# A two-layer convolutional attention kernel: the piece of the next projections moved ahead of the first turned tile

## The reference, cut to what matters

```python
xs = x.reshape(b, c, seq).transpose(0, 2, 1)
qkv = xs @ Wqkv + bqkv
q, k, v = jnp.split(qkv, 3, axis=-1)
...
scores = jnp.einsum('bhqd,bhkd->bhqk', q, k) / jnp.sqrt(jnp.asarray(HEAD_SIZE, x.dtype))
attn = jax.nn.softmax(scores, axis=-1)
out = jnp.einsum('bhqk,bhkd->bhqd', attn, v)
...
x = x + _L0_conv_ref(_gn(x), L0_conv_Wqkv, L0_conv_bqkv, L0_conv_Wout, L0_conv_bout)
x = x + _L1_conv_ref(_gn(x), ...)
```

## Time and profile before

| | |
|---|---|
| median of 3 runs | 3008.57 us (3002.29 to 3011.41) |
| the profiled execution, its own time | 3005.0 us |
| its span, from the first to the last instruction | 3003.2 us |
| mean granted clock of TensorE | 0.971 |
| busy share of PE, DVE, ACT, POOL | 92%, 73%, 55%, 7% |
| share of the chain that ended last: PE, DVE, ACT, DMA | 73%, 12%, 5%, 4% |

### The profile page before, as it was taken

How to read it: one execution, slowest core, us unless ns; L and a number is a source line. 1 busy time by engine, 2 the same in 40 slices (tenths; PEclk the granted TensorE clock), 3 DMA queues, 4 the chain that set the end, 5 groups by cost and what they waited for, 6 DMA issues and landing times.

```text
span 3003.2 us, 60746 instructions
## 1 busy us (share of the span) xinstructions
PE 2771.4 (92%) x25208; PEld 1948.6 (65%) x25208; DVE 2201.0 (73%) x2934; ACT 1665.8 (55%) x2429; POOL 197.3 (7%) x157
## 2 busy tenths in 40 slices
PE   6999799999999999999999999999999999998858
PEld 5666576756667577665776667765677756765434
DVE  5676577687875877868877778768787588775856
ACT  2653466375653755636665556636566375554625
POOL 0000001000200002000020000200020000200300
PEclk9999899999999999999999999999999999998968
DMA  5233012421233112340224311232123311105040
GB/s 202 66 74 107 36 43 76 135 81 45 59 95 130 48 54 60 89 174 8 65 59 134 113 43 39 80 130 86 45 52 101 131 48 54 38 12 175 13 110 29
DMA packets 149602, 235.85 MB, mean 79 GB/s; under 512 B 78609, under 2 KB 97556, under 8 KB 145460
## 3 DMA queue, kind: packets, MB, share of 16 engines
q1 hardware_dynamic: 148468, 219.39, 23.7%
q10 hardware_dynamic: 864, 12.58, 1.2%
HBM read 177.08 MB, written 54.84 MB: 77 GB/s over the span
## 4 chain that ended last, share of the span: by engine, by line
PE 73%; DVE 12%; ACT 5%; DMA 4%; issue 4%; another core or an unknown queue 1%; SPq 0%; DVEq 0%; POOL 0%; ACTq 0%
PE banks L708 12%; PE banks L648 10%; PE banks L677 9%; PE banks L695 8%; PE banks L638 6%; PE banks L894 5%; PE banks L750 5%; PE banks L904 4%; PE banks L896 4%; PE banks L895 4%; DMA recips_dram<-recips 3%; DVE neg_max L1432 3%; DVE exps_turned L1443 2%; ACT exps L1111 2%; PE banks L867 2%
## 5 line engine op out<-in xcount | busy, mean ns | idle before, releaser
L1432 DVE TENSOR_REDUCE neg_max<-banks 128x1 f32<-128x1024 f32 x512 | 601.8, 1217 | 88.8 <-PE banks L677 86.0
L1111 ACT ACTIVATE exps<-banks,neg_max 128x1024 f32<-128x1024 f32 x512 | 566.8, 1113 | 47.4 <-DVE neg_max L1432 46.3
L1123 ACT ACTIVATE exps_turned<-banks 128x1024 f32<-128x1024 f32 x256 | 262.3, 1025 | 553.2 <-PE banks L695 544.9
L1443 DVE COPY exps_turned<-banks 128x1024 f32<-128x1024 f32 x256 | 313.2, 1223 | 262.3 <-PE banks L695 247.5
L677 PE MATMUL banks<-qk_halves 64*128 64x512 f32 x3072 | 432.9, 412 | 60.7 <-ACT exps L1111 39.6
L708 PE MATMUL banks<-exps_turned,values 128*64 128x256 f32 x4096 | 481.1, 384 | 0.8 <-issue 0.8
L695 PEld LDWEIGHTS banks<-ident,exps 64*128 64x128 f32 x8192 | 311.5, 139 | 199.1 <-issue 171.3
L695 PE MATMUL banks<-ident,exps 64*128 64x64 f32 x8192 | 366.6, 228 | 31.4 <-DVE exps_turned L1443 27.3
L708 PEld LDWEIGHTS banks<-exps_turned,values 128*64 128x64 f32 x4096 | 280.3, 137 | 138.8 <-issue 5.1
L677 PEld LDWEIGHTS banks<-qk_halves 64*128 64x128 f32 x3072 | 292.4, 189 | 109.9 <-issue 75.8
L1613 DVE SCALAR_TENSOR_TENSOR qk_halves<-banks,qk_halves 128x1024 fp32r<-128x1024 f32 x256 | 302.0, 1219 | 67.2 <-ACT qk_halves L1160 66.9
(11 more groups left out here) (187 smaller groups left out, 3388.9 us busy)
## 6 DMA issues: line engine op xcount, KB each, us to landing
wqk_ring<-wqk_split SPq DMA_DIRECT2D x62, 512.0 KB
wo_halves<-wo_split_dram SPq DMA_DIRECT2D x8, 2048.0 KB, 7.8
exps_turned<-in_x SPq DMA_DIRECT2D x32, 512.0 KB, 5.6
x_dram<-exps SPq DMA_DIRECT2D x32, 512.0 KB, 2.6
exps_turned<-x_dram SPq DMA_DIRECT2D x32, 512.0 KB, 6.0
out<-exps_turned SPq DMA_DIRECT2D x32, 512.0 KB, 2.6
recips_b<-recips_dram SPq DMA_DIRECT2D x240, 64.0 KB, 3.4
x_image<-in_x SPq DMA_DIRECT2D x14, 1024.0 KB, 7.0
```

The lines of the kernel that those rows point to most:

```text
L1111: freed(act.activation(PB[:, 2 * h + n % 2], slot(("s", m, i)), ACT.Exp, bias=NM[:, m:m + 1], accum_out=SS[:, m:m + 1]), ("s", m, i))
L1432: dve.tensor_reduce(NM[:, m:m + 1], slot(("s", m, i)), AX.X, ALU.max, negate=True).then_inc(mx, 1)
L1443: dve.tensor_copy(PT[:, n // 2 % 2, 1, :, P * j:P * j + P].rearrange("p k (r q) -> p k r q", r=2), TB.rearrange("p r (k q) -> p k r q", k= ...
```

## The change

In the loop over steps on PE, the two lines that issue the piece of the next projections move up: they stood behind the first turned tile and the value products, and now stand between the scores and the first turned tile. Nothing else is edited.

```diff
                     elif i + 1 < B:
                         values(0, i + 1)
+                    if piece_of(n + 1):
+                        piece(n + 1, i)
                     turn(n, 0, i)
                     if n == 0:
                         piece(0, i)
...
                     if (2 <= n < 22 and n % 2 == 0) or (n > 22 and n % 2):
                         value_product(n // 2 - 1, 1, i)
-                    if piece_of(n + 1):
-                        piece(n + 1, i)
                     if i and n == 25:
```

## The result

The changed kernel takes 3300.64 us, the median of four runs (3297.57 to 3303.23); the kernel before took 3005.43 us on the same chip in four runs (2989.46 to 3011.41). The ratio is 1.0988, with an interval of 1.0964 to 1.1013: 10% slower. The prediction said 3338 us. The profiled execution took 3303.23 us, with a span of 3301.4 us and a mean granted clock of 0.942, against 0.971 before.

A forecast was written before the change was run, and what follows sets the result against it. In steps with a piece, PE's order and ACT's copy-exp-exp chain were taken to bound the kernel, ending together. 259.6 - 14.2 + 4 = 249.4; 3005.0 + 249.4 + 84 for clock falls = 3338 us, range 3250 to 3380.

The forecast's parts named there:

- The step itself: In 88 steps with a piece, the first turned tile and ACT's work come 2.95 us later: 8.67 for 5.72, 259.6 us added.
- The two waits: PE waits 1.22 us for ACT's copy and 1.47 us for the exps in each changed step, at no further cost.
- What is given back: In 20 steps the piece covers the first turned tile's wait for DVE's copy: 14.2 us off, bounds nothing and 27.3.
- The piece's wait for its bank: In step 1 of each image the piece waits about 0.5 us for DVE's low part: 4 us added.
- The falls of the clock: TensorE's clock falls to half in 55 of 88 changed steps, at 1.52 us each: 84 us, bounds 0 and 134.
- the eight cases behind it: Earlier places in the trace with like waits on PE: five of eight fell, 0.63, the share taken for the 88 steps.
- bound by PE's own 6.37 us: The step after one with a piece is set by PE's order at 6.37 us, so DVE's 0.37 us gain stays hidden.
- the prediction's own signs of being wrong: ACT's exps starting before the copy's end, the piece running beside the transposes, or even steps taking under 6.37 us.
- The rival of a give-back: Row maxima bound the following step; their earlier start returns 0.37 us in each of 88, falls hide: 3221 us, chance 0.07.
- The rival without falls: The two waits, split by a turned tile, bring no fall of TensorE's clock: 3254 us, chance 0.18.

## Why the prediction was right

The sign and the mechanism were right. The time lies inside the range, 37 us below the value given. Point by point:

- *The step itself.* 8.67 us was predicted, 8.63 measured. ACT's order is the cause: with the exps ahead of the copy the scores' wait is gone, and with half of the piece moved the delay is half. The first turned tile came 4.52 us behind the scores (894.84 to 899.36), 0.04 us earlier than 1.61 + 2.95.
- *The two waits.* Predicted 1.22 and 1.47 us, measured 1.21 and 1.48; in total 110.0 against 3 + 107 for the copy, 165.9 against 39.6 + 129 for the exps.
- *What is given back.* 14.2 us of the waits for DVE's copy was predicted, 16.2 came (27.3 to 11.1). The piece's wait for its bank was put at 4 us, and is 4.9.
- *The falls of the clock.* 55 of 88 at 1.52 us was predicted. In 54 of 88 the scores behind a piece took over 1.75 us. Of the 73 following steps with a whole value product and no work of the second layer on PE, 27 took 6.21 us or less and 46 took 7.59 or more, and these 46 are the ones with slow scores. The typical ones differ by 7.72 - 6.20 = 1.52 us. That the falls are the cause was shown by filling the waits: 78, 84 and 76 us come back (81, 87 and 79 when each kernel is taken against the kernel before on its own chip), against 54 x 1.52 = 82. That the share came out so near, 55 and 54, is luck: of the eight cases behind it only one had the two waits of a changed step, and the experiments show that one wait of this length behind a piece brings no fall.
- *The term that was mis-sized.* The prediction took the following step as "bound by PE's own 6.37 us" and so gave back nothing there. At full clock it takes 6.20 us after the change: 0.17 x 88 = 15 us less. This is one of the prediction's own signs of being wrong, an even step below 6.37 us. With both waits filled, where there are no falls, the steps behind a piece add up to 550.2 us, 19.4 less than before; 2.6 of these are waits for DVE's copy that went. The two chains of the earlier trace rows do not end exactly together, as the prediction read them. The scores at 820.01 were recorded as starting before the turned tile ended at 820.20; this part of their time is PE's excess over ACT's chain, and the first 0.17 us of the delay cost nothing. With half a piece left out the excess goes too, and brings 0.19 us per step. The rival of a give-back was right on this, but at half its size and not for its reason: it had named DVE's row maxima and 0.37 us, and a following step whose slack hides a fall. But PE shows no idle time inside the following step at full clock (888.64 to 894.84), so the row maxima do not bound it, and no fall was hidden.

The sum over the timeline of the two profiled executions closes it. The 88 steps with a piece went from 522.2 to 765.2 us, 243.0 more where 249.4 was predicted. The steps behind them went from 569.7 to 630.8, 61.1 more where 84 was predicted: 80.6 for the falls, less the 19.4 given back. The rest of the program took 5.9 us less, where nothing was predicted; the cause of that is open. Together this is 298.2 us, the difference of 3303.2 and 3005.0; predicted were 333.

The rival without falls named a rule of the Trainium skill, in "TensorE: Matmul & The Clock Gate", section "HAM oscillation — how this bites in real kernels", that the clock falls back when TensorE pauses for long. Taken to mean that shorter pauses bring no fall, it gave 3254 us. Taken so, the trace disagrees with it: there are 54 falls behind waits of 1.21 and 1.48 us.

## What to carry to other kernels

A piece of work that can stand in several places on PE is best put where it covers a wait that PE has anyway and delays nothing that another engine's queue stands behind. Here it covered ACT's copy between two turned tiles; ahead of the first of them it delayed a copy, and with it two exps that didn't need the copy but stood behind it in ACT's order. When two engines' chains look equally long in a profile, take work from one and see how little the time falls: that tells the slack of the other (0.19 us a step here), which a delay may use before it costs. And a wait on PE that is uncovered close to another wait can have a second price, so look at the granted clock in the steps behind it.

## What the runs showed of the hardware that was not expected

Matmuls whose result nobody uses made the changed kernel faster. Five of them (1.43 us) in each of the 88 steps took it from 3300.6 to 3216.8 us (beside kernels before of 3005.4 and 3008.3), since TensorE stayed at the higher level of its clock there: the mean granted clock was 0.971, after 0.942.

The share of falls was taken mostly from single waits of 1.58 us. In the steps with a piece they came with two waits: 54 of 88 with 1.21 and 1.48 us around a turned tile of 0.71 us, none of 88 with either wait alone behind a whole piece. Longer single waits brought a fall twice, 2.99 us behind half a piece and 4.48 us with the exps first; one of 2.33 us brought none. Why some of the 88 fall and others don't was not settled.
